# Experts' tiles from slot 5 of the last batch's step, and an opening in which ScalarE writes the zeros and sends part of the first transfers

## The reference

```python
mod = (silu(c) @ wmod).reshape(16, 6, 1, 128)
sa, ca, ga, sb, cb, gb = mod parts; ga, gb = sign * max(abs, 0.25)
x = x + ga * attention(layernorm(x) * (1 + ca) + sa)     # 16 heads of 8, rotary, causal softmax
h = layernorm(x) * (1 + cb) + sb
probs = softmax(h @ router.T); top 2 of 8 experts, shares made to sum to 1
y = sum over the two of share * (gelu_tanh(h @ w_fc[e] + b_fc[e]) @ w_proj[e] + b_proj[e])
x = x + gb * y
```

## Time and profile before

| what | us |
|---|---|
| median of 3 runs | 555.8 |
| lowest and highest | 553.67, 558.47 |
| profiled execution, its own time | 555.56 |
| its span (first to last instruction) | 553.8 |
| PE busy | 453.2 (82%) |
| DVE busy | 401.1 (72%) |
| POOL busy | 346.9 (63%) |
| ACT busy | 300.3 (54%) |

### The profile page before, as it was taken

The page is one execution under the profiler, slowest core; times in us unless marked ns, Lnnn a source line. Parts: engine busy times, 40 slices in busy tenths (PEclk is TensorE's granted clock), DMA queues, the critical chain, the costliest instruction groups (busy, mean ns, idle before and its releaser), DMA issues.

```text
span 553.8 us, 12554 instructions
## 1 busy us (share of the span) xinstructions
PE 453.2 (82%) x3543; PEld 334.8 (60%) x3543; DVE 401.1 (72%) x1194; ACT 300.3 (54%) x836; POOL 346.9 (63%) x483
## 2 busy tenths in 40 slices
PE   2567999889989889888988989689869679999940
PEld 1334556555655555555655655369859669999940
DVE  6757898899999799999999799635335424444763
ACT  1104565565555455555555555657647348878730
POOL 5655554556976856966966857825656554444872
PEclk9869999999999899999999999989999789999985
DMA  5145445635745725754745852422222322224723
GB/s 150 41 109 161 141 125 126 169 93 145 217 127 153 218 88 146 216 146 131 226 128 125 188 156 55 131 55 64 64 64 68 86 56 69 70 68 138 229 81 117
DMA packets 77731, 68.40 MB, mean 123 GB/s; under 512 B 10403, under 2 KB 71079, under 8 KB 77664
## 3 DMA queue, kind: packets, MB, share of 16 engines
q1 hardware_dynamic: 72160, 58.08, 38.3%
q0 software_dynamic: 4320, 8.47, 4.6%
q10 hardware_dynamic: 1184, 1.05, 0.6%
HBM read 25.98 MB, written 12.05 MB: 69 GB/s over the span
## 4 chain that ended last, share of the span: by engine, by line
PE 33%; DVE 31%; issue 11%; SPq 6%; DMA 5%; POOL 5%; another core or an unknown queue 4%; ACT 2%; DVEq 1%; POOLq 0%
DVE maxima L1379 10%; PE ps_sc L1545 8%; PE ps_max L1555 4%; PE ps_pv L1555 4%; DMA k_diags<-k_stacks 4%; PE misc L1706 3%; SPq L553 3%; PE ps_pv L1662 3%; DVE shifts L1393 2%; PE ps_max L1615 2%; DVE turned_b L1330 2%; DVE stats L978 2%; DVE z L993 2%; SPq L521 2%
## 5 line engine op out<-in xcount | busy, mean ns | idle before, releaser
L895 ACT ACTIVATE probs<-ps_sc 128x512 f32<-128x512 f32 x192 | 110.0, 596 | 79.6 <-PE ps_sc L1633 51.1
L1379 DVE TENSOR_REDUCE maxima<-ps_max 128x2 f32<-128x512 f32 (+1 forms) x192 | 130.5, 682 | 25.4 <-PE ps_max L1617 12.9
L749 POOL DMA_INDIRECT results<-after_k,after_e x71 | 70.1, 987 | 69.7 <-DVE after_k L1076 44.7
L759 POOL TENSOR_SCALAR_AFFINE_SELECT probs<-probs 128x512 f32<-128x512 f32 x128 | 82.1, 645 | 38.4 <-ACT probs L895 36.9
L1633 PE MATMUL ps_sc<-q_diags,k_stacks 128*128 128x512 f32 x192 | 96.5, 504 | 6.1 <-ACT probs L895 4.8
L1545 PE MATMUL ps_sc<-x_in,after_k 128*128 128x128 f32 x568 | 79.9, 286 | 18.5 <-ACT x_in L865 8.7
L859 ACT ACTIVATE after_k<-ps_sc,after_k 128x128 f32<-128x128 f32 x284 | 89.5, 373 | 0.3 <-PE ps_sc L1545 0.3
L1545 PEld LDWEIGHTS ps_sc<-x_in,after_k 128*128 128x128 f32 x568 | 72.5, 200 | 19.9 <-ACT x_in L865 13.8
L709 POOL DMA_INDIRECT sorted_rows<-rows,slots x64 | 65.4, 1022 | 14.5 <-issue 10.0
L1615 PE MATMUL ps_max<-k_diags,q_stacks 128*128 128x512 f32 x128 | 62.3, 486 | 0.7 <-DVE maxima L1379 0.7
L1662 PE MATMUL ps_pv<-probs,v_wides 128*32 128x256 f32 (+1 forms) x1024 | 56.2, 338 | 1.3 <-POOL probs L759 1.3
(11 more groups left out here) (181 smaller groups left out, 877.0 us busy)
## 6 DMA issues: line engine op xcount, KB each, us to landing
k_diags<-k_stacks SPq DMA_DIRECT2D x64, 128.0 KB
q_diags<-q_stacks SPq DMA_DIRECT2D x64, 128.0 KB
gate_now<-gate_rows SPq DMA_DIRECT2D x16, 320.0 KB
after_e<-sorted_rows SPq DMA_DIRECT2D x71, 65.0 KB
k_stacks<-high SPq DMA_DIRECT2D x32, 128.0 KB
q_stacks<-high SPq DMA_DIRECT2D x32, 128.0 KB
x_in<-in_x SPq DMA_DIRECT2D x16, 128.0 KB
k_stacks<-low SPq DMA_DIRECT2D x16, 128.0 KB
```

The lines of the kernel that those rows point to most:

```text
L749: nc.gpsimd.indirect_dma_start(result_dram, bass.IndirectOffsetOnAxis(ap=row_in[m % RING][:, D + 1:D + 2].bitcast(U32), axis=0), y_out[m % ...
L759: nc.gpsimd.affine_select(four, four, [[0, 4], [1, P]], ALU.is_ge, 0.0, base=0, channel_multiplier=-1).then_inc(S["causal_done"], 1)
L895: nc.scalar.activation(probs[:, g % 2, c], ps_sc[u % 2][:], ACT.Exp, scale=SCALE).then_inc(S["exp_done"], 1)
L1379: nc.vector.tensor_reduce(to, of, AX, ALU.max).then_inc(S["max_done"], 1)
```

## The change

TILES_AT becomes 5: tile 0 stands in slot 5 of step 16 and the steps hold 19 tiles. To make that possible banks and buffers move: the up products go to misc[2] and ps_max[1] instead of ps_sc; the down products of tiles 0 to 4 go to misc[0] and later ones to ps_sc (before: ps_max[1] and ps_pv); y_bias gets memory of its own; first_tile on PE waits for the last shifts and the attnT copy instead of for all exponentials, on DVE for the last maxima instead of the last scores. The eight sorts of pair 5 are all put into step 15 (SORT_CLOSE_AT).

In the opening ScalarE takes over most zeros: `clear` copies a zero tile (q_stacks[:, 1]) over the target. Seven (four of k_diags, three of q_diags) stand after step -2, the rest (`clear_late`) in slot 6 of step -1. `first_transfers`, ahead of clear_late in ScalarE's program, issues the three q_stack transfers of batch 0 and two of its four k_diag transfers. The gate matmuls move from before step -1 to its slot 3.

```diff
-TILES_AT = 9
+TILES_AT = 5
+Y_SPARE = 5
+SORT_CLOSE_AT = {2: (0, 0), 3: (0, 1), 4: (0, 2), 5: (0, 3), 7: (1, 0), 8: (1, 1), 9: (1, 2), 10: (1, 3)}
...
-        y_bias = [x_in[1][:, 0, :], x_in[1][:, 1, :], x_res[0][:, 0, :]]
+        y_bias_all = next_free(3 * D).rearrange("p (n d) -> p n d", n=3)
...
-        ps_y = [ps_max[1], ps_pv]
+        up_bank = [misc[2], ps_max[1]]
         def y_bank(m):
-            return ps_y[0] if m < 2 else ps_y[m % 2]
+            return misc[0] if m < Y_SPARE else ps_sc[m % 2]
...
                 def stack_q_high():
-                    if s.has(1):
+                    if s.has(1) and s.t >= 0:
...
-                        for w in range(4):
+                        for w in range(2 if s.t == -1 else 4):
...
             def clear_rest():
-                nc.gpsimd.memset(shifts[:].bitcast(F32), 0.0).then_inc(S["zeroed"], 1)
-                nc.gpsimd.memset(v_wides[:], 0.0).then_inc(S["zeroed"], 1)
-                pool.wait_ge(S["zeroed"], 10)
+                nc.gpsimd.memset(chosen[:], 0.0).then_inc(S["zeroed"], 1)
+                pool.wait_ge(S["cleared"], 10)
                 for n in range(2):
                     nc.gpsimd.memset(v_wide[n][:, :, :, DK:DK + 1], 1.0).then_inc(S["zeroed"], 1)
-                nc.gpsimd.memset(chosen[:], 0.0).then_inc(S["zeroed"], 1)
-                nc.gpsimd.memset(k_stacks[:, 1:3].bitcast(F32), 0.0).then_inc(S["zeroed"], 1)
-                for g in range(GROUPS):
-                    nc.gpsimd.memset(q_diags[:, 0, g].bitcast(F32), 0.0).then_inc(S["zeroed"], 1)
-                for g in range(GROUPS):
-                    nc.gpsimd.memset(k_diags[:, 1, g].bitcast(F32), 0.0).then_inc(S["zeroed"], 1)
...
-                    if s.sorts() and s.t < B and n in SORT_AT:
+                    if s.sorts() and s.t < B - 1 and n in SORT_AT:
                         sort_some(s, *SORT_AT[n])
-                    if s.routes() and s.t <= B and n in SORT_LATER_AT and s.pair >= 1:
+                    if s.t == B - 1 and n in SORT_CLOSE_AT:
+                        sort_some(s, *SORT_CLOSE_AT[n])
+                    if s.routes() and s.t < B and n in SORT_LATER_AT and s.pair >= 1:
...
-            for g in range(GROUPS):
-                nc.gpsimd.memset(k_diags[:, 0, g].bitcast(F32), 0.0).then_inc(S["zeroed"], 1)
...
+            def clear(dst):
+                nc.scalar.activation(dst, q_stacks[:, 1].rearrange("p g t -> p (g t)").bitcast(F32), ACT.Copy).then_inc(S["cleared"], 1)
...
+            def first_transfers():
+                act_e.wait_ge(S["high_done"], 2)
+                for n in range(2):
+                    act_e.dma_start(way(q_stack[0], n), high[:, 0, :].bitcast(F32)).then_inc(S["stacked"], 16)
+                act_e.wait_ge(S["low_done"], 2)
+                act_e.dma_start(way(q_stack[0], 2), low[:, 0, :].bitcast(F32)).then_inc(S["stacked"], 16)
+                act_e.wait_ge(S["k_stacked"], 48)
+                act_e.wait_ge(S["ones_in"], 16)
+                act_e.wait_ge(S["cleared"], 4)
+                for w in (2, 3):
...
+                    if s.t == -1 and n == 6:
+                        first_transfers()
+                        clear_late()
...
-            steps(emit)
+            emit(Step(-2))
+            clear_early()
+            steps(emit, -1)
...
-                dve.wait_ge(S["score_mm"], UNITS * B)
+                dve.wait_ge(S["max_done"], UNITS * B)
...
-                if m == 3:
-                    pe.wait_ge(S["heads_done"], B * 4)
+                if m == Y_SPARE:
+                    pe.wait_ge(S["exp_done"], B * UNITS)
...
-                pe.wait_ge(S["exp_done"], B * UNITS)
+                pe.wait_ge(S["shift_out"], B * 4)
+                pe.wait_ge(S["attn_t_done"], B - 1)
...
+                    if n == 3 and s.t == -1:
+                        gates()
...
-            for n, j in enumerate((2, 5, 4, 3)):
-                last = nc.tensor.matmul(ps_max[1][0:B, n * D:(n + 1) * D], c_silu[:], wmod_s[:, j * D:(j + 1) * D],
-                                        start=True, stop=True)
-            last.then_inc(S["gate_mm"], 1)
```

More of the change, by code:

```diff
@@ L378, in block_program @@
         sums = next_free(4 * T).rearrange("p (n a d) -> p n a d", n=4, a=TILES)
+        y_bias_all = next_free(3 * D).rearrange("p (n d) -> p n d", n=3)
+        y_bias = [y_bias_all[:, n] for n in range(3)]
         y_sum = [sums[:, n] for n in range(2)]
@@ L822, in emit @@
                         sort_by_tile(m - 1)
-            emit(Step(-2))
-            for g in range(GROUPS):
-                nc.gpsimd.memset(k_diags[:, 0, g].bitcast(F32), 0.0).then_inc(S["zeroed"], 1)
-            steps(emit, -1)
+            steps(emit)
             def final(b):
@@ L870, in gelu_and_turned, with clear_early, clear_late @@
                     turned_out(m + 2)
+            def clear(dst):
+                nc.scalar.activation(dst, q_stacks[:, 1].rearrange("p g t -> p (g t)").bitcast(F32), ACT.Copy).then_inc(S["cleared"], 1)
+            def clear_early():
+                act_e.wait_ge(S["zeroed"], 4)
+                for g in range(GROUPS):
+                    clear(k_diags[:, 0, g].rearrange("p w t -> p (w t)"))
+                for g in range(GROUPS - 1):
+                    clear(q_diags[:, 0, g].rearrange("p w t -> p (w t)"))
+            def clear_late():
+                clear(q_diags[:, 0, GROUPS - 1].rearrange("p w t -> p (w t)"))
+                for n in range(2):
+                    clear(v_wides[:, n].rearrange("p a h r -> p (a h r)"))
+                for n in range(1, 3):
+                    clear(k_stacks[:, n].rearrange("p g t -> p (g t)"))
+                nc.scalar.activation(shifts[:].rearrange("p n a t -> p (n a t)"), q_stacks[:, 1, 0:2].rearrange("p g t -> p (g t)").bitcast(F32),
+                                     ACT.Copy).then_inc(S["cleared"], 1)
+                for g in range(GROUPS):
+                    clear(k_diags[:, 1, g].rearrange("p w t -> p (w t)"))
+            def first_transfers():
+                act_e.wait_ge(S["high_done"], 2)
+                for n in range(2):
+                    act_e.dma_start(way(q_stack[0], n), high[:, 0, :].bitcast(F32)).then_inc(S["stacked"], 16)
[5 more added lines that the diff above has]
+                for w in (2, 3):
+                    at = slice(ROWS * w, ROWS * (w + 1))
+                    act_e.dma_start(k_diag[0][at, :, w, :].bitcast(F32), k_stack[0][at].bitcast(F32)).then_inc(S["k_spread"], 16)
             def gap_exponential(s):
@@ L1544, in up @@
                 for hc in range(HC):
-                    last = nc.tensor.matmul(ps_sc[m % 2][:, hc * P:(hc + 1) * P], staged[m % 3][:, hc * P:(hc + 1) * P],
+                    last = nc.tensor.matmul(up_bank[m % 2][:, hc * P:(hc + 1) * P], staged[m % 3][:, hc * P:(hc + 1) * P],
                                             row_t[m % 2], start=True, stop=True)
@@ L1728, in fill, with gates @@
                             rank(s.pair, bank)
+                def gates():
+                    for n, j in enumerate((2, 5, 4, 3)):
+                        last = nc.tensor.matmul(ps_max[1][0:B, n * D:(n + 1) * D], c_silu[:], wmod_s[:, j * D:(j + 1) * D],
+                                                start=True, stop=True)
+                    last.then_inc(S["gate_mm"], 1)
                 for n in range(UNITS):
+                    if n == 3 and s.t == -1:
+                        gates()
                     if s.has(0):
```

34 lines of the change are left out of this document (18 added, 16 removed).

## The result

The kernel after took 557.6 us (median of 19 runs) against 554.9 for the kernel before beside it: ratio 1.005, 95% interval 1.0026 to 1.0073. It is slower by half a per cent, where I had forecast 553.3 us, faster by half a per cent. The profiled execution has a span of 555.5 us against 553.8 before. That is one execution each, and executions of one kernel scatter (548.8 to 558.5 us in the 19 of the kernel before), so the medians say how much slower it is and the profiles only where.

A forecast was written before the change was run, and what follows sets the result against it. PE was taken as nearly always busy except in the opening and where tiles begin. Opening -7.5 us and tiles about +5 gave -2.5: 555.8 to 553.3 us; range 546 to 560.5, the forecast's own 549 to 558.

The forecast's parts named there:

- (2): Opening: the four gate matmuls move behind kr and qr, where PE was idle anyway; saves 1.85 us.
- (4): Opening: first k and q transfers shared over two queues, 7.1 us from low to scores instead of 8.9; saves 1.8 us.
- (1): Opening: DVE's c_den takes 0.2 us instead of 3.45 without POOL's memsets beside it; 2.15 us arrive.
- (3): Opening: DVE's z at 0.6 us and low at 0.5 us, so low's first half comes 1.8 us earlier.
- (5): Step 0: ScalarE's late clears, about 7.9 us, end before its next work there, high; hidden by 1.3 us.
- (6): Opening: PE's lower clock left unchanged; if it stayed up, at most 3.0 us would come on top.
- (7): Tiles at slot 5 of step 16: first up matmuls 4.5 us earlier; pair 5's moved sorts cost 0.5 us.
- (8): First tiles: ScalarE alternates exp and gelu, six more table loads (7.7 us), all in the loop; tiles +4.7 us.
- (9): After tile 4: same order, last sort and load 41 hidden; unknown waits of 19.8 us kept whole, +-3 us.
- C: Opening's gain eaten by late clears or stretched landings, down to 3 us: 557.8 us; chance 0.10.
- B: Slots 5 to 8: every table switch costs a drain too, 7.7 us more: 561.0 us; chance 0.14.
- A: First tiles: ScalarE's table loads run in PE's idle time, so 4.5 us arrive: 543.8 us; chance 0.17.

The follow-up runs named there:

- the opening half: Kernel before with only the opening's part of the change, tiles at slot 9 (opening_only); ratio to before 0.9888, on another chip 0.992, both without the waits.
- open_warm: The opening half with the gates' matmuls and nine idle transposes filling TensorE's gap before the permuted tables; ratio to the kernel before 0.9894.
- open_sp_transfers: The opening half with the first transfers of q and k all on SP again; ratio to the kernel before 0.9933.
- after_tanh: Kernel after with tanh in place of the tiles' gelu, so no table is loaded among the tiles; ratio to the kernel before 0.9994.
- tiles_only: Kernel before with only the tiles' part: tiles at slot 5, banks moved, pair 5's sorts in step 15; ratio to before 1.0289, chip without the waits.
- after_2: Kernel after, unchanged, run once more on a chip without the waits; ratio to the kernel before 1.0189.
- after_pack_2: Kernel after with the last pair's eight sorts two to a send, repeated on a chip without the waits; ratio to the kernel before 1.0075.
- after_here: Kernel after, unchanged, run again on a chip with the waits; ratio to the kernel before 1.0044.
- after_pack: Kernel after with the last pair's eight sorts two to a send, on a chip with the waits; ratio to the kernel before 1.0103.
- open_gap_gates: The opening half with the gates' matmuls put in TensorE's gap before the permuted tables, on a chip with the waits; 550.9 us.

## Why the prediction was wrong

The forecast was 2.5 us faster; the change is 2.7 us slower by the medians and 1.7 by the two profiled spans. In the spans the sum is off by 4.2 us: 2.4 in the opening, 2.6 in the steps, which had no term, and 0.8 the other way in the tiles. The step that failed most clearly is the opening's sum of 7.5 us, in (2) and (4): it gave 5.1.

The runs on one chip with the waits price the halves without the profiles. The two variants of the opening half stand at 0.9943 and 0.9933 there and the kernel after at 1.0044. So the opening gives 3.2 to 3.7 us (each known to 2 us) and the tiles half costs 5.6 to 6.2 (to 3 us), which is 2.4 us slower in sum. The tiles' +5 was near that; the 7.5 was twice what arrived.

**(1), c_den:** right; 0.17 us and 1.83 of the 2.15 us, since in_sin, for which the permutes wait, took 5.74 us to land instead of 5.4.

**(2), gates behind kr and qr:** half right. kr starts at 13.42, near the forecast 13.3. The step "kr and qr (2.41 us)" took its duration from one profile, in which 1.89 us of other matmuls ran just before. It measured 3.61 us: 1.2 us lost. With the old opening it was 2.41 and 2.01 us, with the new one never under 2.41 and in the middle 3.3, so the term was too small for the new place. Why stays open: open_warm's 1.95 us after unbroken work fits the pause as the cause, but the scatter of the others with the same pause is nearly as large.

**(3), z and low:** nearly right. z took 1.07 us instead of 0.6, low 0.90 for both halves. All that comes before the first transfer gained 4.45 us of 5.8.

**(4), the transfers:** mis-sized. The spread was costed at 1.35 us of issue and a landing of 2.0 to 2.5, so at most 3.85 from its first issue to the scores; it took 4.57 (22.89 to 27.46), with 3.68 for the last landing. The whole of (4) gave 0.65 us instead of 1.8, of which the sharing is 0.5 (open_sp_transfers). The opening gave 5.1 us instead of 7.5, just outside my bounds of 5.5 to 8.5.

**(5), late clears:** right, hidden. **(6), the clock:** nothing came of it, but not for the reason given. The granted clock was at 0.50 (1.2 GHz) until 30.5 us and 0.95 from there to 31, three microseconds after work had resumed at 27.46 instead of six; step 0 still took 18.13 us against 17.89.

**(7), first up matmul:** 3.6 us earlier instead of 4.5. **(8), the switches:** right in kind, with luck in the size. The turns took 4.9 to 5.8 us against 4.85. A turn was added up from ScalarE's work alone, but PE's down matmuls and scores take as long as the copy and the load in front of an exponential: from the end of gelus 1 at 367.09 to the scores at 368.61 it is 1.52 us, and copy and load were 1.53 in the sum. So not all seven loads are "in the loop". Gelus 3 ended 4.8 us late instead of 3.0, tile 8 was weighed 6.7 us late, and the end came 4.2 us late, against +5; the 2.5 us between the last two came back in the waits of (9), for which the sum had nothing. Over the profiles, tile 8 comes 4.5 to 9.9 us later than in the layout at slot 9 on the same kind of chip. after_tanh shows that it is the loads.

**(9), "Hidden":** wrong in its argument, and saved by the chip. I compared the last sort with load 41 by a pace that was taken from the trace of before, in which the waits give GpSimd its time. Where they are missing, GpSimd is behind by up to 7.6 us (the longest lag of a send behind its weighing in tiles_only), and the four further sends ahead of the last sort cost 4.4 us at tile 41 (after_2, and nothing in after_pack_2). So the change costs 1.9% there and 0.4 to 0.5% where I had read the trace. The same step kept the unknown waits whole, at 19.8 us +-3; their share of the chain went from 29.1 to 20.9%, which is 14.2 us, and the tiles 8 to 40 from 86.8 to 84.2 us. That helped the kernel after by 2.6 us and made up for part of (8), in this profile; in after_here the same stretch took 86.1 us.

**The steps** got 0 in my sum and show +2.6. The other kernels lie from 294.4 to 299.3 us there (tiles_only 297.9), the three profiles of the kernel after from 300.0 to 300.7. after_pack, whose steps are the same program as those of the kernel after, took 294.4. Over all profiles the nine with tiles at slot 5 have a mean of 298.0 us and the ten others 297.0, and each group scatters by 4 to 6 us. So the +2.6 may be chance, and no run decides it; it stays open.

Of the rivals, C (the opening's gain down to 3 us, 557.8 us) gave nearly the number. Its gain is near the 3.2 to 3.7 us of the ratios and under the 5.1 of the profile; of its reasons the stretched landing was there, (5) was not. B's drain was not there. A's reason, that the loads run in idle time, held for two of seven and was wrong in the main, since taking them away gives 8 to 12 us up to tile 8. D's clock was not kept up: it was at 0.50 from 22 to 30.5 us.

## What to carry to other kernels

Don't take the price of a moved matmul from one profile of its old place: the same eight took 2.0 to 3.6 us in this kernel's first 20 us. Price a transfer that is shared out over a second queue with its landing, not its issue alone. When work starts earlier against a queue that does not, write down for every producer in that queue how many entries now stand ahead of it, and compare at the pace of the best chip and not at that of the trace. And start work that needs another activation table only behind the last use of the old one: five of the seven loads stood in the loop with their full 1.28 us. Before adding up one engine's work as a loop, check which of its pieces run beside another engine's.

## What the hardware did that I had not expected

Chips of one kind differ by 3.7% on the same kernel (534.3 to 535.5 us on three, 554.2 to 555.8 on the others), and nearly all of it lies in the tiles with indirect sorts (84 to 89 us against 66 to 74 from tile 8 to 40): without those sorts a chip that took 554.2 us for the kernel before ran the opening half in 528.7, like the others (528.2, 528.0). What in the sorts holds up PE's signals there is not shown, nor that the sorts alone do it. By an estimate from 550.9 us (open_gap_gates) and 528.7, moving them out from among the tiles would be worth up to 4% on such chips, eight times what this change was about; no run tried it.

The best kernel of this study that computes the reference is the opening half alone: 0.9888 and 0.992 on two chips, with variants of it at 0.9943 and 0.9933 on a chip with the waits. open_warm, at 0.9894, can't be told from it.
